# Rotating the latent keys and values once, during the first MoE, instead of batch by batch inside latent attention

## The reference

```python
x = x + tanh(g_xattn[0]) * L0_xattn(layernorm(x), ctx_512, ...)   # causal attention
x = x + tanh(g_ffn[0])   * L0_ffn(layernorm(x), ...)              # MoE, 8 experts, top 1, and a shared expert
x = x + tanh(g_xattn[1]) * L1_xattn(layernorm(x), ctx_512, ...)   # latent attention, below
x = x + tanh(g_ffn[1])   * L1_ffn(layernorm(x), ...)              # attention and MoE, 32 experts, top 8

def L1_xattn(hidden_q, kv_c, Wq, w_kc_q, w_kc_kv, W_qr, W_kr, Wo):
    q_hk  = (hidden_q @ Wq.T).reshape(B, S, H, K)                 # 16 heads
    q_big = rope(einsum('bshk,hkq->bshq', q_hk, w_kc_q), sin_q, cos_q)
    kv_r  = kv_c * cos_k + rotate_half(kv_c) * sin_k              # 8 x 1444 x 64
    q_r   = einsum('bshq,hqr->bhsr', q_big, W_qr)
    k_r   = einsum('bld,hdr->bhlr', kv_r, W_kr)
    attn  = softmax(einsum('bhsr,bhlr->bhsl', q_r, k_r))
    ctx_c = einsum('bhsl,bld->bhsd', attn, kv_r)
    ctx   = einsum('bhsd,hkd->bhsk', ctx_c, w_kc_kv)
    return ctx.reshape(B, S, H * K) @ Wo.T
```

## Time and profile before

| | |
|---|---|
| device time, median of 3 runs | 1550.4 us (1540.61, 1550.4, 1554.96) |
| profiled execution, span | 1563.7 us |
| PE busy | 1450.8 us (93%), 7635 matmuls |
| PE weight loads | 1100.7 us (70%) |
| DVE busy | 935.0 us (60%) |
| ACT busy | 630.5 us (40%) |
| POOL busy | 789.6 us (50%) |
| DMA, mean over the span | 57 GB/s |

### The profile page before, as it was taken

How to read it: one execution, slowest core, us unless ns; L and a number is a source line. 1 busy time by engine, 2 the same in 40 slices (tenths; PEclk the granted TensorE clock), 3 DMA queues, 4 the chain that set the end, 5 groups by cost and what they waited for, 6 DMA issues and landing times. The chain is left out here.

```text
span 1563.7 us, 21601 instructions
## 1 busy us (share of the span) xinstructions
PE 1450.8 (93%) x7635; PEld 1100.7 (70%) x7635; DVE 935.0 (60%) x1619; ACT 630.5 (40%) x1151; POOL 789.6 (50%) x621
## 2 busy tenths in 40 slices
PE   7788999899989999999999998988999998899998
PEld 4455566566646676676766755567988887899998
DVE  2752112466686768767686753577878774444554
ACT  2432221344423434424244342456666653333333
POOL 3732002367647769768677673057565551233332
PEclk9998999799999899989989999999999999999999
DMA  8014113510011101011010000101010001443441
GB/s 306 1 44 142 34 38 86 179 53 24 1 39 57 58 0 58 1 58 58 1 57 7 14 1 14 71 28 33 23 55 1 28 1 42 120 119 120 121 121 52
DMA packets 60321, 88.66 MB, mean 57 GB/s; under 512 B 7556, under 2 KB 44612, under 8 KB 60230
## 3 DMA queue, kind: packets, MB, share of 16 engines
q1 hardware_dynamic: 59206, 85.82, 17.2%
q0 software_dynamic: 1024, 1.64, 0.4%
HBM read 81.92 MB, written 5.41 MB: 56 GB/s over the span
## 5 line engine op out<-in xcount | busy, mean ns | idle before, releaser
L1007 ACT ACTIVATE prob<-PS 121x800 f32<-121x800 f32 x192 | 158.1, 837 | 254.0 <-PE PS L2041 238.3
L1405 DVE TENSOR_REDUCE mx<-PS 128x1 f32<-128x482 f32 (+1 forms) x312 | 186.7, 649 | 56.6 <-PE PS L2019 54.6
L622 POOL TENSOR_TENSOR e_wl<-e_wf,e_wh 128x768 fp32r<-128x768 f32 x33 | 71.0, 2151 | 174.4 <-ACT e_wh L905 152.6
L717 POOL TENSOR_TENSOR hT<-hT,prob 121x800 f32<-121x800 f32 x56 | 109.7, 1958 | 71.1 <-ACT prob L1007 68.9
L2018 PE MATMUL PS<-kth,qs 128*128 128x482 f32 (+1 forms) x312 | 131.5, 422 | 13.7 <-DVE mx L1405 10.3
L2056 PE MATMUL PS<-prob,kvn 121*64 121x400 f32 (+1 forms) x768 | 136.1, 503 | 0.9 <-ACT prob L1007 0.9
L717 POOL TENSOR_TENSOR xc<-xc,prob 121x800 f32<-121x800 f32 x56 | 114.8, 2050 | 30.3 <-ACT prob L1007 25.8
L2019 PE MATMUL PS<-kl,qm 66*128 66x482 f32 (+1 forms) x312 | 125.4, 402 | 0.0
L2038 PE MATMUL PS<-qs,kth 128*121 128x400 f32 (+1 forms) x384 | 113.1, 377 | 3.1 <-ACT prob L1007 2.4
L2041 PE MATMUL PS<-qm,kl 66*121 66x400 f32 (+1 forms) x384 | 105.4, 357 | 0.0
L2056 PEld LDWEIGHTS PS<-prob,kvn 121*64 121x64 f32 (+1 forms) x768 | 52.3, 137 | 71.2 <-issue 69.0
(11 more groups left out here) (301 smaller groups left out, 3650.1 us busy)
## 6 DMA issues: line engine op xcount, KB each, us to landing
e_wb<-routing SPq DMA_DIRECT2D x32, 400.0 KB, 3.9
wgu<-in_L_ffn_gate_up_proj SPq DMA_DIRECT2D x8, 1024.0 KB, 14.3
krt<-in_ctx_T SPq DMA_DIRECT2D x8, 722.0 KB, 4.1
ksw<-in_ctx_Tswap SPq DMA_DIRECT2D x8, 722.0 KB, 5.8
wdn<-in_L_ffn_down_proj SPq DMA_DIRECT2D x8, 512.0 KB, 7.9
wq<-in_L_ffn_Wq SPq DMA_DIRECT2D x4, 1024.0 KB, 5.3
wo<-in_L_ffn_Wo SPq DMA_DIRECT2D x4, 1024.0 KB, 5.7
e_wf<-in_L_ffn_Wg SPq DMA_DIRECT2D x32, 128.0 KB, 2.2
```

Source lines behind the costliest of these rows:

```text
L622: pool.tensor_tensor(m["wl"][:, slot], m["wf"][:, slot], m["wh"][:, slot].bitcast(fp32), ALU.subtract).then_inc(ms["wlo"], 1)
L717: pool.tensor_tensor(acc, acc, prob[:, n % RING], ALU.add).then_inc(xb["ap"], 1)
L1007: act.activation(prob[0:k, n % RING], PS[0:k, 2 * (n % 2):2 * (n % 2) + 2, 0:GC], ACT.Exp).then_inc(xb["ex"], 1)
L1405: dve.tensor_reduce(mx3[:, m, g:g + 1], PS[:, 4 + k % 3, 0:SEG[g][1]], AX.X, ALU.max).then_inc(xb["free"], 1)
```

## The change

The rotation of all batches' keys and values, and the split of the keys, move into the first MoE's tile loop, through two new tables in HBM, `keys_d` (4 pairs of batches x high and low x 128 x 1444) and `values_d` (8 x 121 x 768).

- Keys lie in pairs of batches on 128 rows (the layout `paired`) where each batch had its 64 rows twice. DVE rotates a pair in two halves of 722 columns (`CH`; two multiplications and an addition each), ACT copies the high part (`high_turned`) over the swapped halves, and DVE subtracts to get the low part (`low_turned`). There is one pair of buffers, `keyx` and `keys_`, which lie in `xc` and `sq`.
- Values are rotated by DVE, three operations of 121 x 768 a batch, in two pairs of buffers, which lie in `htok` and `back`, the buffers of scatter and gather. `kcosN` lies in `rstd`.
- DVE's list: pair `k` at tiles 3k to 3k + 2 of the loop, values 0 to 3 there too, values 4 to 7 with tiles 12 and 13.
- POOL's list, between scatters and gathers: all loads and stores of these tables, in the order of the code below. SP's list gets the loads of the four tables of cosines and sines at the end of the first norm, where it had them in the query stage.
- In the query stage SP waits until all stores are complete and then loads batches 0 and 1 from the new tables. In keys and scores it loads keys two batches ahead (`kth`, `kl2` get three buffers) and values one ahead. All rotations, `high_keys` and `low_keys` go from there. DVE sets the ones rows of all three `kl2` at the stage's start, and TensorE's first unit waits for all three.
- The additions of the probabilities stay with the engines that had them.

```diff
+        kcosN = rstd[0:KP, 0:KT * DC]
+        keyx, keys_ = (t_.rearrange("p c t -> p (c t)")[:, 0:SK] for t_ in (xc, sq))
+        valx = [t_[0:KP, 0:KT * DC] for t_ in (held0, held1)]
+        vals_ = [t_[0:KP, KT * DC:2 * KT * DC] for t_ in (held0, held1)]
...
-        kth = sb("kth", [P, 2, SK], fp32r, stack=st3)
-        kl2 = sb("kl2", [DC + 2, 2, SK], fp32r, stack=st3)
+        kth = sb("kth", [P, 3, SK], fp32r, stack=st)
+        kl2 = [sb(f"kl{i}", [DC + 2, SK], fp32r, stack=st) for i in range(2)]
+        kl2.append(sb("kl2", [DC + 2, SK], fp32r, stack=st3))
...
# SP, end of the first norm
+            for tab, src in ((kcosT, "rope_kcosT"), (ksinT, "rope_ksinT")):
+                sp.dma_start(tab[:], a[src]).then_inc(rk["tab"], 16)
+            for tab, src in ((kcosN, "rope_kcosN"), (ksinN[:], "rope_ksinN")):
+                sp.dma_start(tab, a[src].rearrange("p t d -> p (t d)")).then_inc(rk["tab"], 16)
...
# SP, query stage, and keys and scores
+            def load_keys(b):
+                half_, ld = slice((b % 2) * DC, (b % 2 + 1) * DC), xb["ldk"][b % 3]
+                for lo in (0, DC):
+                    sp.dma_start(kth.bitcast(fp32)[lo:lo + DC, b % 3, :], keys_d[b // 2, 0, half_, :]).then_inc(ld, 16)
+                sp.dma_start(kl2[b % 3].bitcast(fp32)[0:DC, :], keys_d[b // 2, 1, half_, :]).then_inc(ld, 16)
             def load_values(b):
+                sp.dma_start(kvn[:, b % 2].rearrange("p t d -> p (t d)"), values_d[b]).then_inc(xb["ldn"][b % 2], 16)
+            sp.wait_ge(rk["st"], 16 * 2 * NP)
+            sp.wait_ge(rk["vst"], 16 * B)
+            for b in range(2):
+                load_keys(b)
+                load_values(b)
...
-                if b + 2 < B:
-                    sp.wait_ge(xb["kl"], 3 * (b + 2))
-                    load_turned(b + 2)
+                if b < 0:
+                    load_keys(2)
+                elif b + 2 < B and b > 0:
+                    sp.wait_ge(xb["s"], SP_ * b)
+                    load_keys(b + 2)
+                if 1 <= b < B - 1:
+                    sp.wait_ge(xb["pv"], 4 * b)
                     load_values(b + 1)
...
# POOL, first MoE, between scatters and gathers
+            def load_turned(k):
+                if k:
+                    pool.wait_ge(rk["st"], 32 * k)
+                pool.dma_start(keyx, a["ctx_T"][k]).then_inc(rk["ld"], 16)
+                pool.dma_start(keys_, a["ctx_Tswap"][k]).then_inc(rk["ld"], 16)
+            def store_turned(k):
+                pool.wait_ge(rk["hi"], RHI + 2 * k + 2)
+                pool.dma_start(keys_d[k, 0], keys_).then_inc(rk["st"], 16)
+                pool.wait_ge(rk["lo"], RLO + 2 * k + 2)
+                pool.dma_start(keys_d[k, 1], keyx).then_inc(rk["st"], 16)
+            def load_natural(v):
+                ld = rk[f"vld{v % 2}"]
+                if v >= 2:
+                    pool.wait_ge(rk["vst"], 16 * (v - 1))
+                pool.dma_start(valx[v % 2], a["ctx_N"][v].rearrange("p t d -> p (t d)")).then_inc(ld, 16)
+                pool.dma_start(vals_[v % 2], a["ctx_Nswap"][v].rearrange("p t d -> p (t d)")).then_inc(ld, 16)
+            def store_natural(v):
+                pool.wait_ge(rk["vrot"], 3 * v + 3)
+                pool.dma_start(values_d[v], valx[v % 2]).then_inc(rk["vst"], 16)
+            load_turned(0)
+            pool.wait_ge(ms0["sc"], 16 * B)
+            load_natural(0)
+            load_natural(1)
+            for k, done_ in enumerate(((0,), (1, 2), (3,), (4, 5, 6, 7))):
+                store_turned(k)
+                if k + 1 < NP:
+                    load_turned(k + 1)
+                for v in done_:
+                    store_natural(v)
+                    if v + 2 < B:
+                        load_natural(v + 2)
+            pool.wait_ge(rk["st"], 32 * NP)
+            pool.wait_ge(rk["vst"], 16 * B)
             for n in range(4):
                 pool.wait_ge(ms0["st"][n], 16 * len(range(n, NT, 4)))
...
# POOL, query stage, and keys and scores
-                if 7 <= u < 25 and u % 2:
-                    rotate_turned(0, (u - 7) // 2)
-                elif u in (25, 27, 29):
-                    rotate_values(0, (u - 25) // 2)
...
-            for n in range(9):
-                rotate_turned(1, n)
...
# ACT, first MoE
+            def high_turned(k, c):
+                act.wait_ge(rk["rot"], 6 * k + 3 * c + 3)
+                act.activation(keys_[:, CH[c]].bitcast(fp32r), keyx[:, CH[c]], ACT.Copy).then_inc(rk["hi"], 1)
             for i in range(NT):
                 tile_gate(i)
                 if i >= 1:
                     keep_hidden(i - 1)
                 if i + 1 < NT:
                     keep_tokens(i + 1)
+                if 1 <= i <= 3 * NP and i % 3:
+                    high_turned(i // 3, i % 3 - 1)
...
# DVE, first MoE
+            def rotate_turned(k, c):
+                if c == 0:
+                    dve.wait_ge(rk["ld"], 32 * (k + 1))
+                dve.tensor_tensor(keys_[:, CH[c]], keys_[:, CH[c]], ksinT[:, CH[c]], ALU.mult).then_inc(rk["rot"], 1)
+                dve.tensor_tensor(keyx[:, CH[c]], keyx[:, CH[c]], kcosT[:, CH[c]], ALU.mult).then_inc(rk["rot"], 1)
+                dve.wait_ge(rk["rot"], 6 * k + 3 * c + 2)
+                dve.tensor_tensor(keyx[:, CH[c]], keyx[:, CH[c]], keys_[:, CH[c]], ALU.add).then_inc(rk["rot"], 1)
+            def low_turned(k, c):
+                dve.wait_ge(rk["hi"], RHI + 2 * k + c + 1)
+                dve.tensor_tensor(keyx[:, CH[c]].bitcast(fp32r), keyx[:, CH[c]], keys_[:, CH[c]], ALU.subtract).then_inc(rk["lo"], 1)
+            def rotate_natural(j):
+                v, x, w = j // 3, valx[j // 3 % 2], vals_[j // 3 % 2]
+                if j % 3 == 0:
+                    dve.wait_ge(rk[f"vld{v % 2}"], 32 * (v // 2 + 1))
+                    dve.tensor_tensor(w, w, ksinN[:], ALU.mult).then_inc(rk["vrot"], 1)
+                elif j % 3 == 1:
+                    dve.tensor_tensor(x, x, kcosN, ALU.mult).then_inc(rk["vrot"], 1)
+                else:
+                    dve.wait_ge(rk["vrot"], j)
+                    dve.tensor_tensor(x, x, w, ALU.add).then_inc(rk["vrot"], 1)
             for i in range(NT):
                 tile_product(i)
                 if i >= 2:
                     keep_output(i - 2)
+                k = i // 3
+                if i == 0:
+                    dve.wait_ge(rk["tab"], RTAB + 64)
+                if k < NP and i % 3 < 2:
+                    rotate_turned(k, i % 3)
+                if k < NP and i % 3 >= 1:
+                    low_turned(k, i % 3 - 1)
+                if k < NP and i % 3 == 1:
+                    rotate_natural(4 * k)
+                if k < NP and i % 3 == 2:
+                    for j in range(1, 4):
+                        rotate_natural(4 * k + j)
+                if i >= 3 * NP:
+                    for j in range(4):
+                        rotate_natural(4 * (NP + i - 3 * NP) + j)
...
# DVE, keys and scores
-            dve.memset(kl2[DC:DC + 2, 0].bitcast(fp32), 1.0).then_inc(xb["one"], 1)
-            for g in range(3):
-                low_keys(0, g)
+            for n in range(3):
+                dve.memset(kl2[n].bitcast(fp32)[DC:DC + 2, :], 1.0).then_inc(xb["one"], 1)
...
-            dve.memset(kl2[DC:DC + 2, 1].bitcast(fp32), 1.0).then_inc(xb["one"], 1)
...
-                    if s == 2 and more:
-                        for g in range(3):
-                            low_keys(b + 1, g)
...
# TensorE, keys and scores
-                if m == 0:
-                    pe.wait_ge(xb["kth"], 3 * b + g + 1)
-                    pe.wait_ge(xb["kl"], 3 * b + g + 1)
                 if u == 0:
-                    pe.wait_ge(xb["one"], min(b + 1, 2))
+                    pe.wait_ge(xb["ldk"][b % 3], 16 * len(range(b % 3, NT, 4)) + 48 * (b // 3 + 1))
+                    pe.wait_ge(xb["one"], 3)
...
-                    pe.wait_ge(xb["nrot"], 3 * (b + 1))
+                    pe.wait_ge(xb["ldn"][b % 2], 16 * len(range(b % 2, NT, 4)) + 16 * (b // 2 + 1))
```

More of the change, by code:

```diff
@@ L16, with flamingo @@
 AX = mybir.AxisListType
-def flamingo(nc, a, out, scratch, sorted_x, sorted_y):
+def flamingo(nc, a, out, scratch, sorted_x, sorted_y, keys_d, values_d):
     P = 128
-    B, S, D = a["ctx_T"].shape[0], a["rope_q"].shape[2], a["xT"].shape[0]
+    B, S, D = a["ctx_N"].shape[0], a["rope_q"].shape[2], a["xT"].shape[0]
     T = B * S
@@ L156, in flamingo @@
         yt = sb("yt", [P, 4, D], stack=st)
-        back = sb("back", [S, B, D], stack=st)
+        held1 = sb("held1", [P, B * D], stack=st)
+        back = held1[0:S].rearrange("p (b d) -> p b d", d=D)
         ssg = sb("ssg", [P, 2, HALF], stack=st)
@@ L284, in flamingo @@
         ms0["back"] = [sem(f"m0_back{i}") for i in range(2)]
+        xb = {k: sem(f"xb_{k}") for k in ("z", "one", "q2", "fill", "free",
+                                          "nmx", "nmh", "qm", "s", "ex", "ap", "ad", "pv", "raw", "sums", "inv", "cx")}
```

(38 more changed lines are left out.)

79 lines of the change are left out of this document (13 added, 66 removed).

## The result

The changed kernel takes 1583.1 us in the median of its four runs (1579.6 to 1584.0), against 1550.4 for the kernel before (1540.6 to 1555.0): a ratio of 1.0222 with a 95% interval of 1.0186 to 1.0258. That is slower by 33 us, and one us above the top of the predicted range. Its profiled execution has a span of 1581.9 us and took 1583.6.

A forecast was written before the change was run, and what follows sets the result against it. TensorE was taken to bound both touched stages. About 24 us lost to DMA round trips in the first MoE, less 17 gained in keys and scores, gave +7 on the 1550.4 median: 1557, range 1534 to 1582.

The forecast's parts named there:

- What is late next is TensorE itself: Keys and scores: without the stalls TensorE sets the pace, six intervals taking 361.8 us instead of 386.1.
- its last rival: Keys and scores: another DVE wait comes in all seven batches at 1.7, about 8 of 24 won, 1566; chance 0.16.
- the wait of the second kind: Keys and scores: TensorE waits while DVE's product (2.20) and addition (2.62) on SBUF operands run during POOL's value rotation.
- POOL has no rotation left at that point: Keys and scores: the argument against 1.7 us waits in all seven batches, since POOL's rotations are moved away.
- The first tile's load shares the engines with 3 MB of first loads: 0 to 2, I take 1.: Start of the first MoE's tile loop: the first tile's load is delayed, costing 1 us.
- The walk through the pairs: First MoE: step-by-step timing of key pairs and values through loads and stores, last output copy ending at 264.4, +23 us.
- the lower estimate beside it, 3.7 and 5.4: First MoE: store 3.7 and loads 5.4 by the Trainium skill's DMA page, with which the stage loses +10.
- VectorE's own way: First MoE: DVE takes 10.6 us from a pair's first multiplication to its last subtraction, gaps included.
- The detour of POOL's order: First MoE: value 2's store and value 4's load precede a key store, so pair 3 starts only at 232.2.
- The ones rows: Start of keys and scores: DVE sets three ones rows before anything else, the first maximum coming 1.5 us later.
- That the round trip is hidden: First MoE: trips of 6.8 us or less fit, the MoE costs 0 to 4, time 1531; chance 0.14.
- That POOL's issue takes 2.6 or more: First MoE: issuing 128 rows of 5.8 KB is slow and shifts every store and load, +49, time 1583; chance 0.20.

The follow-up runs named there:

- experiment 9: The changed kernel, with POOL's slice-5 addition waiting for VectorE's last addition of the half before: 1563.8 us, 1.0126 of the kernel before.
- experiment 1: The kernel before, unedited, profiled a second time: 1537.9 us, span 1536.2.
- experiment 3: The changed kernel without its first-MoE work, and with VectorE's last addition of a half at slot 2 instead of 5: 1529.6 us, 0.9885 of the kernel before.
- 2: The changed kernel without its first-MoE work, attention loading one key pair for all batches and unrotated values: 1549.6 us, 1.0021 of the kernel before.
- 8: The changed kernel with early first loads, key pairs spread four tiles apart, and VectorE's last addition at slot 2: 1530.3 us, 0.9899 of the kernel before.
- 7: The changed kernel with early first loads, first pair rotated during the shared expert's products, others four tiles apart: 1549.4 us, 1.0013 of the kernel before.
- experiment 5: The changed kernel with all first-MoE operations on the first loads' data, without later loads and with one store at the end: 1556.8 us, 1.0072 of the kernel before.
- Experiment 4: The changed kernel with the loads of the first key pair and value 1 issued ahead of the scatters: 1571.1 us, 1.0142 of the kernel before.
- experiment 6: The changed kernel with value 2's store and value 4's load behind the third key store and last key load: 1578.6 us, 1.0206 of the kernel before.

## Why the prediction was wrong

The forecast was 1557 from two terms: 24 lost in the first MoE, 17 won in keys and scores. Measured: 33.6 lost, and nothing won.

**The step that failed first: "What is late next is TensorE itself".** With the stalls on the maxima gone, six intervals were to take 361.8 us; the changed kernel's take 373.7. Late next was VectorE's last addition of a half. In the changed kernel's timelines of VectorE, POOL (the three additions together, then the second and the third alone) and TensorE:

```profile
761.52 2.51 DVE L1476 TENSOR_TENSOR xc<-xc,hT 121x800 f32<-121x800 f32 x1
...
759.25 6.54 POOL L739 TENSOR_TENSOR xc<-xc,prob 121x800 f32<-121x800 f32 x3 [2.86 <-ACT prob L1018]
...
761.29 1.89 POOL L739 TENSOR_TENSOR xc<-xc,prob 121x800 f32<-121x800 f32 x1
...
763.33 2.46 POOL L739 TENSOR_TENSOR xc<-xc,prob 121x800 f32<-121x800 f32 x1
...
764.18 0.89 PE L2098 MATMUL PS<-xc,ones 121*64 121x400 f32 x4 [1.77 <-DVE xc L1476]
```

The addition takes 2.51 where 0.98 would do, beside three POOL additions that run one after the other, and TensorE loses 1.77 in each of six batches. It begins 0.23 us behind the second POOL addition and ends 0.85 behind that one's end (763.18), and POOL's third addition then takes 2.46 instead of 1.89. This is the rule that the prediction took from the Trainium skill (SBUF — State Buffer, Who interferes with whom): a Vector instruction with two inputs in SBUF contends with a GpSimd instruction that reads SBUF, and of two that contend the one that issues first fully blocks the other. The prediction's sentence left out who issues first; the trace agrees with both directions, and experiment 9 shows that the POOL addition is the cause: with POOL held back there, the addition takes 0.98 and the waits sum to 1.5 us instead of 10.7.

The prediction had this as its last rival (a wait at 1.7 in all batches, 8 of 24 won, chance 0.16), but looked for it at the wait of the second kind, the product and the addition that stand ahead of the maxima, and answered it with "POOL has no rotation left at that point". That answer was beside the matter: POOL's additions were enough, and they stayed. The wait of the second kind did not come (0.2 us on the maxima in all); that the wait at the other place is about as long as the rival's 1.7 is chance.

Before, the same addition stood beside the same POOL additions and cost TensorE only 0.9 us in three waits (1.7 in six in experiment 1). The traces show why: it began later within a POOL addition. In this batch of the profile before it began 0.6 us ahead of that one's end and ended 0.86 behind it:

```profile
540.65 1.89 POOL L717 TENSOR_TENSOR xc<-xc,prob 121x800 f32<-121x800 f32 x1 [2.34 <-ACT prob L1007]
...
541.92 1.48 DVE L1438 TENSOR_TENSOR xc<-xc,hT 121x800 f32<-121x800 f32 x1
```

In other batches, and in the first six of experiment 1, it began some 0.15 ahead of the end and took about 1.0. In the changed kernel it begins just behind the start of the next. So half a microsecond made a short addition a long one; what moved the two against each other was not tried.

**The rival's price was too low as well.** It left 8 of the gain, and the runs left nothing. Without that wait the part in keys and scores is worth 16.6 us (experiment 3), almost the 17 of the forecast, and the intervals take 356.3, even below the 361.8. The wait is 10.7, but taking it away wins 20.0 and 19.1 where both kernels ran side by side (experiment 3 against 2, 8 against 7), and 373.67 - 356.34 = 17.3 in the six intervals. The rest is the slow clock behind it. Behind the first two of the six, at 574.17 and 640.20, the granted clock is below 1, behind the later ones not (columns as in the earlier trace rows):

```profile
580.00:590.00 10.00, 10.00 (x40) 5.23 (x39) 6.37 (x10) 1.60 (x2) 1.88 (x1) 0.71 0.00 0
...
636.00:646.00 10.00, 8.21 (x33) 6.12 (x32) 6.60 (x9) 3.30 (x5) 5.50 (x3) 0.83 0.00 0
...
761.00:771.00 10.00, 8.23 (x41) 5.58 (x41) 8.41 (x13) 3.02 (x4) 6.39 (x4) 1.00 0.00 0
```

The intervals that hold these two are 66.0 and 62.9 us, the other four 61.2 to 61.3; experiment 3 has 59.3 to 59.5 in all six.

**The term that was mis-sized: "The first tile's load shares the engines with 3 MB of first loads: 0 to 2, I take 1."** It was 8.3, 156.93 - 148.59. Some 2 of it came ahead of the loads: the last scatter was issued at 145.50, before at 143.54. With the same issues ahead of it the last scatter is at 143.32 in experiment 5, and what made it late was not tried. The other 6.3 are the DMA engines' work: 3 MB at the 304 KB a us of the working are 10 us, and the tile's load was issued in their midst, at 148.22. The bytes stood in the sentence; the division was not made. Experiment 4 got 9.4 back.

**What held.** The walk through the pairs was right but for that shift, as the rows of the first section show: the pairs' first multiplications were expected at 181.1, 204.0 and 232.2 and came at 190.5, 211.7 and 240.9, the last output copy's end at 264.4 and came at 273.2: late by 9.4, 7.7, 8.7 and 8.8. A round trip was put at 12.3 from the last subtraction on and took 190.47 - 177.68 = 12.8 and then 211.74 - 200.11 = 11.6; the lower estimate beside it, 3.7 and 5.4, would have been 9.1. VectorE's own way, put at 10.6, was 9.6 for the second pair. The detour of POOL's order was put at 28.2 - 22.9 = 5.3 and was 29.2 - 21.3 = 7.9 (experiment 6). The query stage was to cost nothing, and from its first matmul to the first ones row it takes 163.6 us (310.78 to 474.36) where it took 163.7. VectorE's operations took what was assumed:

```profile
L1322 DVE TENSOR_TENSOR sq<-sq,ksinT 128x722 f32<-128x722 f32 x8 | 7.2, 906 | 30.2 <-DMA sq<-in_ctx_Tswap 30.2
...
L1342 DVE TENSOR_TENSOR held<-held 121x768 f32<-121x768 f32 x8 | 7.7, 957 | 0.2
```

0.90 and 0.95 expected, 0.906 and 0.957 measured, and that they cost only some 1 us themselves is experiment 5. The tail came 1.3 later than the last copy allows: the gathers followed it by 4.0, not 2.7, behind the last value's store. The ones rows were to cost 1.5; TensorE's wait for them is 3.2, against 0.9 for the low keys before, so 2.3.

**The other rivals.** That the round trip is hidden (chance 0.14) fell with the idle times of 7.8 to 14.3. That POOL's issue takes 2.6 or more (0.20) fell as well: the issue of 128 rows of 5.8 KB took 0.62 and less, little over half of the scatter's 1.01. The rival's time, 1583, was met by other causes.

**How the numbers add up.** 1557, plus 17 that were not won, plus 7 for the first tile, plus 1 to 2 for the tail: 1583. That the range missed by one us is small; that its middle was reached by a gain that did not exist is not. A chance of 0.16 for the wait in attention was too low for a rule that the prediction had just seen to agree with the trace.

## What to carry to other kernels

When work is taken off a shared resource, list who still uses it there and which instruction waits next, and price that one too: a POOL addition on SBUF operands held a VectorE addition until it ended, and half a microsecond in when it began decided over 1.5 us. A small move in the order (experiment 3) may be worth as much as the whole rewrite. A round trip through one buffer needs a period, not only enough idle time: way plus trip was 21.3 us where three tiles gave 17.4, and at four tiles, with the first loads ahead of the rush, nearly all of it was hidden. And a small load issued among large ones can be late by a good part of the time that their bytes take: here by 6 us, where 3 MB take 10, though the large ones came from another engine's queue.

## What the runs showed of the hardware

- DMAs with plain rows that POOL issues cost it 0.53 to 0.62 us each in the changed kernel, less than its indirect ones (1.00 to 1.24).
- A VectorE addition of 121x800 with both inputs in SBUF that begins beside a POOL addition of the same size ended 0.85 us behind that one's end, whenever it began: 1.0 us in all when it began 0.15 ahead of that end, 1.48 at 0.6 ahead, 2.51 at 1.7 ahead. POOL's next addition then took 2.46 instead of 1.89.
- While POOL's 3 MB of loads ran, the DMA engines were busy throughout (share 1.01) at 347 GB/s, and a tile of 128 KB that SP issued among them came 6 us late, beside the 2 of its own later issue.
- The clock does not fall behind every idle time of TensorE: of six of 1.76 to 1.79 us in the changed kernel the first two were followed by a granted clock of 0.71 to 0.83 and four by 1.00. The same kernel before had a mean clock of 0.964 in one execution and 0.982 in another, with 27.5 us between their spans. What decides was not found.
